# A bias moved from a TensorE product to an add on GpSimd, with a rearranged start and one store moved forward

## The reference, cut to what matters

```python
# layer 0: one of three networks, chosen by the sequence's condition
out_nr  = gelu(x @ w1_nr  + b1_nr)  @ w2_nr  + b2_nr       # condition 0
out_tsr = gelu(x @ w1_tsr + b1_tsr) @ w2_tsr + b2_tsr      # condition 1
h       = gelu(x @ w1_sr  + b1_sr)                         # condition 2, 512 wide
out_sr  = gelu(h @ w2_sr + b2_sr) @ w3_sr + b3_sr
x = layernorm(x + out_of_the_condition) * gamma + beta
# layer 1: an adapter of 64 units, whose middle matrix is chosen by the domain
hidden = gelu(x @ down_W.T + down_b)
hidden = hidden @ expert_W[domain].T + expert_b[domain] + domain_emb[domain]
x = layernorm(hidden @ up_W.T + up_b + x) * ln_gamma + ln_beta
```

## Time and profile before

| what | us |
|---|---|
| median of 3 runs | 293.97 |
| lowest and highest of them | 293.71, 295.15 |
| the profiled execution | 294.8 |
| its span | 293.0 |

### The profile page before, as it was taken

The page is one execution under the profiler, slowest core; times in us unless marked ns, Lnnn a source line. Parts: engine busy times, 40 slices in busy tenths (PEclk is TensorE's granted clock), DMA queues, the critical chain, the costliest instruction groups (busy, mean ns, idle before and its releaser), DMA issues.

```text
span 293.0 us, 8411 instructions
## 1 busy us (share of the span) xinstructions
PE 267.2 (91%) x2053; PEld 255.3 (87%) x2054; DVE 197.2 (67%) x669; ACT 203.5 (69%) x451; POOL 149.4 (51%) x164
## 2 busy tenths in 40 slices
PE   6879999999999999899999999999999999998410
PEld 6669999999999998799999999999999999997310
DVE  7486623426744844778888788888788887878360
ACT  3157687867777683887878888878878788776100
POOL 3211724734746654556655566545656455562450
PEclk9997999999999999999999999999999999999955
DMA  6561210110221122123242332423223332311121
GB/s 200 138 198 26 57 36 2 41 39 10 47 72 37 49 59 55 35 72 81 71 111 78 88 81 69 101 81 98 73 70 101 86 99 72 92 38 45 57 66 36
DMA packets 44029, 21.00 MB, mean 72 GB/s; under 512 B 37783, under 2 KB 42182, under 8 KB 44008
## 3 DMA queue, kind: packets, MB, share of 16 engines
q1 hardware_dynamic: 41142, 13.95, 19.7%
q0 software_dynamic: 1584, 4.33, 4.1%
q10 hardware_dynamic: 1282, 2.45, 2.8%
HBM read 12.02 MB, written 8.65 MB: 71 GB/s over the span
## 4 chain that ended last, share of the span: by engine, by line
PE 80%; issue 7%; DMA 4%; DVE 3%; POOL 2%; ACT 1%; ACTq 1%; POOLq 1%; DVEq 0%
PE ps_h L943 18%; PE ps_z L1012 10%; PE ps_u L1058 9%; PE ps_d L1067 9%; PE ps_z L1017 5%; PE ps_z L978 5%; PE ps_t L1029 5%; PE ps_u L978 4%; PE ps_t L1116 3%; PE ps_t L1117 3%; PE ps_z L1000 3%; PE ps_t L1119 3%; DMA w_sr_sb<-in_w_sr 2%; DMA out<-o,out_rows_now 1%; PE ps_u L912 1%
## 5 line engine op out<-in xcount | busy, mean ns | idle before, releaser
L446 POOL TENSOR_TENSOR h_lo<-h,h_hi 128x256 fp32r<-128x256 f32 (+1 forms) x75 | 69.7, 930 | 95.6 <-ACT h L805 95.5
L451 POOL TENSOR_TENSOR rs<-ve,minus_half 128x4 f32<-128x4 f32 x36 | 40.9, 1135 | 26.7 <-DVE ve L642 26.6
L805 ACT ACTIVATE h_hi<-ps_h,per_feature_sb 128x256 fp32r<-128x256 f32 x84 | 38.2, 479 | 20.3 <-PE ps_h L943 20.1
L630 DVE BATCH_NORM_STATS2 st<-ps_z 128x6 f32<-128x256 f32 x66 | 24.8, 414 | 33.1 <-PE ps_z L1017 33.1
L812 ACT ACTIVATE zn<-ps_z,nm,rs 128x256 f32<-128x256 f32 x66 | 33.7, 561 | 9.1 <-DVE nm L646 8.5
L461 POOL DMA_INDIRECT out<-o,out_rows_now x33 | 34.9, 1057 | 9.3 <-issue 6.1
L805 ACT ACTIVATE h<-ps_h,per_feature_sb 128x256 f32<-128x256 f32 x84 | 38.0, 481 | 0.0
L829 ACT ACTIVATE yt<-ps_t,per_feature_sb 128x256 f32<-128x256 f32 x66 | 34.0, 573 | 5.2 <-PE ps_t L1029 5.1
L1058 PE MATMUL ps_u<-table_hi,stack 128*128 x132 | 36.5, 306 | 0.0
L1067 PE MATMUL ps_d<-yt,per_feature_sb 128*128 128x256 f32 x132 | 34.1, 380 | 1.3 <-ACT yt L829 1.3
L1058 PE MATMUL ps_u<-table_lo,stack_hi 66*128 x132 | 33.7, 285 | 0.0
(11 more groups left out here) (153 smaller groups left out, 694.8 us busy)
## 6 DMA issues: line engine op xcount, KB each, us to landing
x<-in_x_feat SPq DMA_DIRECT2D x130, 64.0 KB
out<-o SPq DMA_DIRECT2D x66, 64.0 KB, 2.0
last_sb<-in_last_w ACTq DMA_DIRECT2D x1, 768.0 KB, 8.7
out<-o,out_rows_now POOLq DMA_INDIRECT x33, 2.7
w_sr_sb<-in_w_sr SPq DMA_DIRECT2D x1, 512.0 KB, 3.5
w_two_sb<-in_w_two SPq DMA_DIRECT2D x1, 512.0 KB, 4.3
w_sr_sb<-in_w_sr ACTq DMA_DIRECT2D x1, 512.0 KB, 6.6
per_unit_sb<-in_per_unit ACTq DMA_DIRECT2D x1, 325.0 KB
```

Of the source, the lines that this page charges most:

```text
L446: pool.tensor_tensor(dst, full, high.bitcast(F32), ALU.subtract).then_inc(ready, 1)
L451: pool.tensor_tensor(RS[p][:, :, :], VE[p][:, :, :], mhalf[:, :].rearrange("p (n t) -> p n t", n=2), ALU.pow).then_inc(rstd, 1)
L805: ins = act.activation(dst[:, m, :], src[m], ACT.Gelu, bias=COL[:, bass.ds(col + m, 1)])
```

## The change: what it does

1. The product of line 1000 and all that prepared its tile are gone. Instead a tile `XB` (two buffers) holds the input plus the bias of the last product; the bias is a value per feature, which in the input's layout is one value per partition. GpSimd makes it with one `tensor_tensor` add of 128x512 per slot (`add_bias`), chosen by the slot's kind through up to three branches. TensorE copies `XB` instead of the input into `ps_z`. The add for slot g+2 stands in GpSimd's step g, and waits for VectorE's stack copy of the step before (`s_made`). Where the next slot has three layers it stands between the first low part and the power; where it has two, ahead of both low parts.
2. SyncE's next input load waits for `x_lo` and for the add, and no longer for TensorE's copy.
3. In the last late step GpSimd issues its store ahead of the power of the step after.
4. The start is rearranged: gelu's table is loaded first; ScalarE issues `w2_sr` and the rest of `per_unit` before anything else but the small early loads, and `last` and the rest of `per_feature` go to SyncE's queue behind the inputs; `w_two_hi` is made right after `w_sr_hi`; two table pairs instead of one come ahead of slot 0's input split; a fourth pair is folded early, in the place of six products that kept TensorE busy.

```diff
-            pool.memset(LBH[:, :].bitcast(F32), 0.0).then_inc(s_lbh_zero, 1)
-            b_sr, _, _, n_slots = bounds(pool)
+            b_sr, b_nr, b_tsr, n_slots = bounds(pool)
...
+            def biased_input(slot, i, p, where):
+                pool.wait_ge(ld_x[p], 16 * G * (i + 1))
+                if where != HEAD or slot >= 2:
+                    pool.wait_ge(xb_used, slot - 1)
+                pool.sem_inc(x_seen, 1)
+                with pool.If(slot < b_sr):
+                    add_bias(SR, p)
+                with pool.Else():
+                    with pool.If(slot < b_nr):
+                        add_bias(NR, p)
...
+            def add_bias(kind, p):
+                col = COL[:, COL_B3 + KC * kind:COL_B3 + KC * (kind + 1)]
+                pool.tensor_tensor(XB[p][:, :, :], XF[p][:, :, :, :].rearrange("p c k t -> p c (k t)"),
+                                   col.unsqueeze(2).to_broadcast([P, KC, N]), ALU.add).then_inc(xb_made, 1)
...
+            def next_input(g, i, p, where):
+                if where == HEAD and g == -1:
+                    biased_input(1, 0, 1, where)
+                else:
+                    for slot in on_slot(pool, g, -2, where, n_slots):
+                        if where != HEAD or g >= 2:
+                            pool.wait_ge(s_made, g - 1)
+                        biased_input(slot, i + 1, p, where)
...
                 with pool.If(g + 1 < b_sr):
                     low(h1l[:, 0:2, :], h1[:, 0:2, :], h1h[:, 0:2, :], h0_full, h0_lo, g + 1)
+                    next_input(g, i, p, where)
                     if not (where == HEAD and g < 0):
                         power(g, p)
                     low(h1l[:, 2:4, :], h1[:, 2:4, :], h1h[:, 2:4, :], h1_full, h1_lo, g + 1)
                 with pool.Else():
+                    next_input(g, i, p, where)
                     for slot in on_slot(pool, g, -1, where, n_slots):
                         low(h2l[:, 0, :], h2[:, 0, :], h2h[:, 0, :], h0_full, h0_lo, g + 1)
...
+                store(g, p, where)
                 if where == LATE:
                     with pool.If(g + 1 >= n_slots):
                         power(g + 1, 1 - p)
-                store(g, p, where)
...
-                    pe.wait_ge(x_lo, g + 2)
+                    pe.wait_ge(xb_made, g + 2)
...
-                pe.matmul(ZP[p][:, :, :], ones2[:, :],
-                          LBH[:, bass.ds(kind * H, H)].unsqueeze(1).to_broadcast([P, TT, H]),
-                          start=False, stop=False)
...
-                    sp.wait_ge(x_used, g + 2)
+                    sp.wait_ge(x_lo, g + 2)
+                    sp.wait_ge(xb_made, g + 2)
```

More of the change, by code:

```diff
@@ L129, in conditioned_layers @@
         XL = [sb(f"x_lo{p}", [P, KC, G, T], F32R) for p in range(2)]
+        XB = [sb(f"x_biased{p}", [P, KC, N]) for p in range(2)]
         h1 = sb("h1", [P, 2 * KC, N])
@@ L364, in _ @@
             load(rows_to_load(1), 1)
+            sp.dma_start(W["last"][:, :], W_DRAM["last"]).then_inc(s_w_in["last"], 16)
+            sp.dma_start(FEAT[:, EARLY_FEAT:], per_feature[:, EARLY_FEAT:]).then_inc(s_norm_in, 16)
             n_slots = bounds(sp)[OTHER]
-            sp.wait_ge(s_lb, 1)
-            sp.wait_ge(s_lbh_zero, 1)
-            for row, half in enumerate((LB_HI, LB_LO)):
-                sp.dma_start(LBH[row:row + 1, :].bitcast(F32), half[:, :].bitcast(F32)).then_inc(s_lb_low, 16)
             sp.wait_ge(s_ct, 1)
@@ L479, in _ @@
                     continue
+                if where == HEAD and g < 0:
+                    biased_input(0, 0, 0, where)
                 for slot in on_slot(pool, g, 0, where, n_slots):
@@ L603, in input_low @@
                                   ALU.subtract).then_inc(x_lo, 1)
-            table_low(0)
+            for j in range(2):
+                table_low(j)
             input_low(0, 0)
@@ L609, in _ @@
             dve.tensor_tensor(CL[:, :], TP[0:TE, 0, :], CH[:, :].bitcast(F32), ALU.subtract).then_inc(s_ct, 1)
-            for j in range(1, EARLY_PAIRS):
+            for j in range(2, EARLY_PAIRS):
                 table_low(j)
@@ L778, in _ @@
                 load_sequence(act, rows[k], 0, G // 2 + k)
-            act.dma_start(W["w2_sr"][:, :], W_DRAM["w2_sr"]).then_inc(s_w_in["w2_sr"], 16)
-            act.dma_start(UNIT[:, EARLY_UNIT:per_unit.shape[1]], per_unit[:, EARLY_UNIT:]).then_inc(s_unit_rest_in, 16)
-            act.dma_start(W["last"][:, :], W_DRAM["last"]).then_inc(s_w_in["last"], 16)
-            act.dma_start(FEAT[:, EARLY_FEAT:], per_feature[:, EARLY_FEAT:]).then_inc(s_norm_in, 16)
             b_sr, _, _, n_slots = bounds(act)
@@ L787, in input_high @@
                 act.copy(XH[p][:, :, :, :], XF[p][:, :, :, :]).then_inc(x_hi, 1)
-            table_high(0)
+            for j in range(2):
+                table_high(j)
             input_high(0, 0, 0)
-            for j in range(1, EARLY_PAIRS):
+            for j in range(2, EARLY_PAIRS):
                 table_high(j)
@@ L930, in _ @@
             pe.wait_ge(s_unit_in, 16)
-            for j in range(EARLY_PAIRS):
+            for j in range(TABLE_BANKS):
                 table_pair(j)
```

73 lines of the change are left out of this document (28 added, 45 removed).

## The result

The changed kernel takes 296.12 us (median of 5 runs, 295.61 to 296.81), the kernel before 294.02 us beside it (293.71 to 295.15). The ratio is 1.0070, with an interval of 1.0055 to 1.0085: slower by 0.7%. The forecast was 293.0 us, 1 us less than before. The profiled execution took 295.73 us with a span of 293.7 us.

The account below looks back on a forecast made before the run. TensorE was taken as the bound, with GpSimd's loop close behind; product -2.3, two-layer steps +3.0, start -1.7 and drain 0 summed to -1.0 us, forecast 293.0 us, own range 291 to 295, 8-in-10 range 286.5 to 298.0.

Parts of the forecast that it names:

- The sum: Whole kernel: -2.3 + 3.0 - 1.7 + 0 = -1.0 us, giving 293.0 us; chance 0.40.
- the start: Before slot 0's second layer: earlier loads and casts win 1.7 us, bounds +1.5 and -4.
- The two-layer steps: 23 later two-layer slots: GpSimd's add makes steps 6.30 us against 6.17, +3.0 us, bounds -5.3 and +7.6.
- the collision: Two-layer steps: the power, issued just behind x_lo, takes 1.40 us instead of 1.04; such a step costs 6.50 or 6.56.
- the loop's length: Two-layer steps: the loop through VectorE and GpSimd takes 12.11 us for two steps, at least 6.06 a step.
- The product in three-layer steps: Nine three-layer slots and the first two-layer slot: TensorE stays the bound, 10 x 0.23 = 2.3 us won.
- the gelu: Start, slot 0 on ScalarE: gelu comes 1.2 us earlier because the cast no longer waits for w2_sr.
- The drain: End of kernel: earlier store gains 0, since TensorE's own stretch replaces the wait; bounds -3.6 and 0.
- The rival with the loads in the inputs' way: Start: early loads delay the inputs and first layer, +1.5 in place of -1.7, 296.2 us; chance 0.08.
- the one on the slower side: Two-layer steps: power and x_lo collide in every step, 6.50 us each, +3.6 in all, 297.6 us; chance 0.18.

Follow-up runs that it names:

- experiment 8: Changed kernel with VectorE's low part of the two-layer weights made later, after slot 1's x_lo and the last layer's low part: 295.16 us, ratio 1.0040.
- experiment 5: Changed kernel with the bias column from a register instead of branches, and the stack-copy wait behind the other two waits: 290.48 us, ratio 0.9871.
- experiment 2: Changed kernel with GpSimd's add cut to 2 columns of each tile from slot 2 on (leaves out computation): 289.61 us, ratio 0.9849.
- experiment 3: Changed kernel with the bias column from a register read ahead of the wait, in place of branches, from slot 2 on: 292.1 us, ratio 0.9937.
- Experiment 11: Changed kernel with GpSimd's power ahead of the first low part in two-layer steps: 295.35 us, ratio 1.0024.
- experiment 4: Changed kernel without GpSimd's wait for the stack copy ahead of the add, branches kept: 322.61 us, ratio 1.0976.
- Experiment 7: Kernel before, with only GpSimd's store put ahead of the late power in the last steps: 294.19 us, ratio 1.0001.
- experiment 1: Kernel before with the rearranged front alone (load and cast order, four early table pairs, no six filler products): 292.9 us, ratio 0.9959.
- experiment 6: Changed kernel with column by register and the add's last wait on the stack's subtraction instead of its copy: 290.78 us, ratio 0.9875.

## Why the prediction was wrong

**The sum.** The forecast was a gain of 1.0 us; the medians show a loss of 2.1. The step that failed is the start, where 1.7 us were counted as won. In the profiled executions the span grew by 0.7 us, and it splits so:

| stretch | forecast | measured |
|---|---|---|
| to slot 1 (start, product twice) | -2.2 | -1.4 |
| slots 1 to 9 (8 products) | -1.8 | -1.1 |
| slots 9 to 32 | +3.0 | +3.1 |
| behind slot 32 | 0 | +0.1 |

The medians grew by 1.4 us more than this. Behind slot 1 there is no room for it: in the three traces with the product the stretch from slot 1 to 9 is 78.70 to 78.74 us and that from 9 to 32 is 141.8 to 142.1, in the changed kernel and experiment 8 they are 77.7 and 144.7 to 144.9. If the other executions have these steps, they make +1.6 to +2.1 us, and about 0 to +0.4 us is left for the start, not -2.2 (an estimate from these rows and the medians; the drain, 29.7 to 30.3 us in these traces, adds some tenths of doubt).

**The two-layer steps: right in kind, and in size partly by luck.** 6.299 us against 6.30, with the alternation of 1.04 and 1.49 us in the power. But the forecast had steps of 5.94 and 6.56 us by turns, a mean of 6.25, and went to 6.30 without a row for the rest; measured are about 6.13 and 6.46. The short step is not TensorE's 5.94: in the one from 188.21 TensorE waits for no other engine, yet is 0.17 us later at the transposes and another 0.11 at line 1021 than in a step of experiment 5. Inside the loop three estimates were off, with both signs: the add 1.035 instead of 1.28 us, the way to it 0.59 (NR) or 0.76 (TSR) instead of 0.5, and from the low part's end to line 1026 0.05 instead of 0.15 us. Experiments 2, 3 and 5 show the loop from both sides: without the add's time, or with 0.55 us less ahead of it, TensorE is the bound at 5.96 us; with 0.3 us less the steps are mixed. What the collision itself costs is not separated. Experiment 11 takes it off the power and wins 0.06 us of the 0.34 that the loop lies above TensorE's own step, but the low parts are then held by 0.22 us. I had put the loop's length at 12.11 us for two steps and the collision on top. In experiment 11 it measures 2 x 6.24 = 12.48, or 12.26 less the 0.22 (an estimate), so a loop without any collision would still lie above TensorE's 11.92.

The Trainium skill, "SBUF — State Buffer", section "Who interferes with whom", says that VectorE and GpSimd share a pair of ports to SBUF, that a VectorE operation with two inputs in SBUF contends there with a GpSimd operation that reads SBUF, and, of VectorE's two-port modes, that whoever issues first gets the pair for the whole instruction. The low parts that were drawn out beside VectorE's splits agree. Two rows do not fit a hold from issue to end. `x_lo`, issued 0.23 us into a power of 1.04 us, took its usual 0.69 us, so that power does not hold the ports to its end. And in experiment 4 the subtraction of the stack started 0.52 us before the add and still ended behind it; why the add, which came second, goes first is not shown.

**The product in three-layer steps: mis-sized.** "10 x 0.23 = 2.3 us are won there" took the whole product as won. TensorE does stay the bound (59.59 of 59.60 us), but from slot 2 on the steps went from 10.45 to 10.30 us, 0.15 in the mean, and the step from slot 1 to 2 did not get shorter at all (10.46; experiment 2 has 10.26). Together that is 1.1 us of 1.8. From the transposes to line 1026 the 0.24 us are won; about 0.1 us are lost behind it. In the kernel after:

```profile
72.34 0.67 PE L1026 MATMUL ps_z<-last_hi,h_lo 128*128 128x256 f32 x4
72.85 0.28 PE L961 MATMUL ps_h<-x_hi,w_sr_hi 128*128 128x256 f32 x1
...
74.27 0.81 PE L1076 MATMUL ps_d<-yt,per_feature_sb 128*128 128x256 f32 x3
```

and in the kernel before:

```profile
74.08 0.63 PE L1017 MATMUL ps_z<-last_hi,h_lo 128*128 128x256 f32 x4
...
75.93 0.38 PE L1067 MATMUL ps_d<-yt,per_feature_sb 128*128 128x256 f32 x1
```

The way to the next group is 1.93 us and was 1.85, a stretch in which TensorE's sequencer takes branches. That the long product had kept the engine fed over them is my reading; no run tested it.

**The start: the step that failed.** "I count only 0.5 us there and 1.2 us for the gelu: 1.7 us" fails twice.

First, the gelu. ScalarE's cast of `w2_sr` without a wait came as forecast (14.52 instead of 17.03 us), but the gelu behind it started only 0.27 us earlier, since the next wait was as long: 2.16 us for TensorE's first layer, which had waited for `x_lo` and then ran at the lower clock. And the wait of 1.75 us that I read the gain from belongs to one execution. Experiment 7 has the start of the kernel before, and there the cast follows without a wait and the gelu waits for TensorE:

```profile
16.01 1.07 ACT L770 CAST w_sr_hi<-w_sr_sb 128x1024 fp32r<-128x1024 f32 x1
18.48 0.84 ACT L805 ACTIVATE h_hi<-ps_h,per_feature_sb 128x256 fp32r<-128x256 f32 x2 [1.40 <-PE ps_h L943]
```

Second, the adds. The forecast priced one of the three adds at the start. The front alone brings slot 1 to 40.11; the changed kernel has two products less (0.46 us) and should be at 39.65, and is at 41.32. So the adds cost 1.7 us in these two traces. The medians agree: 296.1 - 292.9 = 3.2 us. The steps behind slot 9 make +2.8 of it, those from slot 1 to 9 make -1.1, and the two products -0.5, which leaves 2.0 us for the adds (an estimate). The rows name what they did: `x_lo` of slot 0 took 1.15 us instead of 0.69 (in experiment 1 also 0.69), the add for slot 1 stood between two low parts that VectorE's splits held up (TensorE idle for 0.91 us), and the third add cost 0.39 us. So the front is worth 1.1 us by the medians, two products 0.5, and the adds take all of it back.

The rival with the loads in the inputs' way did not come: `x_hi` of slot 0 was cast at 12.97, before at 13.68.

**The drain: right.** VectorE's copy of the store rows comes at 272.63, not 275.74, without the wait for the store, and TensorE's late stretch takes its place:

```profile
277.83 1.05 PE L996 MATMUL ps_u<-ident,yt 128*128 128x128 f32 x4 [3.79 <-DVE n L689]
```

The row names VectorE's `n`, but that had ended at 277.01; line 996 comes 13.96 us behind slot 32's product and did so before (14.01), so what TensorE does in that time is not shown. From there VectorE's last statistics wait for it, 3.55 us now and 0.45 before. Experiment 7 gives 1.0001.

**What stays open.** The two profiled executions differ by 0.9 us and the medians by 2.1. The profiled execution of before was 0.8 us above its median, and its slot 0 at 31.68 was late: experiment 7, with the same start, had it at 30.88. I read my gain at the start from that late one. Slot 1 is at 42.74 and 41.94 us in the two traces with the old start; with the changed start and the adds it is at 40.87 to 42.06 in six (the kernel after, experiments 3, 4, 5, 6 and 11), 41.37 in the mean. From 41.94 the changed kernel's gain to slot 1 is only 0.6 us. Where executions of one kernel lose or win up to a microsecond before slot 0 (the input's landing, the place of the low clock) is not settled. Of the rivals, the one on the slower side had the sign and not the mechanism: the collision in every step did not come.

## What to carry to other kernels

Before work goes to an engine that has idle time, add up the loop that closes through it, from the wait to the engine that is waited for, and not its busy share: GpSimd was 58% busy in that stretch and yet had only 0.4 us to spare. What the sequencer does between a signal and the operation (branches, register loads, further waits) belongs to that loop, and is the cheapest part to move out of it. Once a loop is shorter, look at the queue that issues the transfers, since it can be the next bound without ever showing as busy. Where a wait is taken out, look for the wait that stands right behind it, and read a gain at the start from more than one execution.

## What the runs showed of the hardware

- An add of 128x512 with a column repeated along the row as second input takes 1.03 to 1.05 us on GpSimd, against 1.28 us for a subtraction of two full tiles of that size.
- A power of 128x4 on GpSimd takes 1.04 us if it is issued 0.02 us or more ahead of VectorE's `x_lo`, an operation with two inputs in SBUF, and 1.44 to 1.60 us if up to 0.2 us behind it. In the same instant both occur (1.60 us in experiment 3, once 1.04 in experiment 8). Issued 0.2 us or so into the power, `x_lo` takes its usual 0.69 us.
- Where an add is ready while GpSimd still issues an indirect DMA, a VectorE subtraction that starts 0.52 us before the add does takes 1.87 us instead of 0.42, and a copy with one input beside the low part behind the add takes 0.72 us instead of 0.29 (experiment 4). The same DMA issue without an add ready behind it does not hold the subtraction (0.42 us beside it at 189.06 in the kernel after).
- SyncE issues one DMA with a row from a register about every 0.78 us (four loads from 150.07 to 153.20 in experiment 5). The gap in which it loads the next 12 registers is 3.2 us; how much of it the load takes is not shown.
